# Two-layer post-LN transformer: the products of two attention steps follow each other, with a third probability buffer

## What is computed

```python
logits = jnp.einsum('btkgh,bskh->bkgts', q * scale, k)        # layer 0
probs = jax.nn.softmax(logits.astype(jnp.float32), axis=-1).astype(logits.dtype)
encoded = jnp.einsum('bkgts,bskh->btkgh', probs, v)
...
scores = jnp.einsum('bnqd,bnkd->bnqk', q, k) * scale          # layer 1
scores = jnp.where(causal, -jnp.inf, scores)
attn = jax.nn.softmax(scores, axis=-1)
out = jnp.einsum('bnqk,bnkd->bnqd', attn, v)
```

## Time and profile before

| | |
|---|---|
| runs | 854.34 us median of 3 (853.07 to 855.31) |
| profiled execution | span 851.4 us from the first to the last instruction; the page gives no other time of it |
| TensorE | 767.9 us busy (90%) |
| VectorE | 446.6 us busy (52%) |
| ScalarE | 359.7 us busy (42%) |
| POOL | 115.4 us busy (14%) |
| DMA | 75.01 MB, mean 88 GB/s |
| attention of layer 0 | first products at 44.9, last at 257.1 us |
| attention of layer 1 | first scores at 508.1, last products at 797.3 us |

### The profile page before, as it was taken

The page is one execution under the profiler, slowest core; times in us unless marked ns, Lnnn a source line. Parts: engine busy times, 40 slices in busy tenths (PEclk is TensorE's granted clock), DMA queues, the critical chain, the costliest instruction groups (busy, mean ns, idle before and its releaser), DMA issues. The chain is left out here.

```text
span 851.4 us, 11512 instructions
## 1 busy us (share of the span) xinstructions
PE 767.9 (90%) x3907; PEld 409.4 (48%) x3908; DVE 446.6 (52%) x1198; ACT 359.7 (42%) x565; POOL 115.4 (14%) x127
## 2 busy tenths in 40 slices
PE   5599999999999999999997879888998989989886
PEld 3222444444435556666665445434464445533675
DVE  2744554565435622222247676868765674662453
ACT  3389775685684012212223233444423442156030
POOL 0000000000000311111842411231011110022000
PEclk9699999999999999999999899989999999999999
DMA  7567207005107161111125870006300370000000
GB/s 217 148 204 223 93 26 209 27 25 149 38 26 247 43 198 46 43 45 46 32 84 169 251 201 2 1 27 187 110 1 3 106 216 1 2 1 26 14 12 26
DMA packets 51582, 75.01 MB, mean 88 GB/s; under 512 B 7607, under 2 KB 44763, under 8 KB 49227
## 3 DMA queue, kind: packets, MB, share of 16 engines
q1 hardware_dynamic: 49660, 69.26, 27.0%
q0 software_dynamic: 1872, 5.11, 2.2%
HBM read 46.57 MB, written 27.66 MB: 87 GB/s over the span
## 5 line engine op out<-in xcount | busy, mean ns | idle before, releaser
L656 PE MATMUL ps<-arena 128*128 128x256 f32 (+3 forms) x1084 | 326.7, 450 | 18.2 <-issue 2.9
L656 PEld LDWEIGHTS ps<-arena 128*128 128x128 f32 x1084 | 201.2, 195 | 106.6 <-issue 68.7
L970 ACT ACTIVATE arena<-ps 128x1024 f32<-128x1024 f32 x128 | 124.2, 1027 | 32.9 <-PE ps L711 32.6
L1067 ACT ACTIVATE arena<-ps 128x1024 f32<-128x1024 f32 (+3 forms) x128 | 82.9, 702 | 114.1 <-PE ps L903 114.0
L1450 DVE TENSOR_REDUCE arena<-ps 128x1 f32<-128x512 f32 (+3 forms) x176 | 100.4, 633 | 28.5 <-PE ps L881 27.6
L769 PE MATMUL ps<-arena 128*128 x184 | 86.5, 593 | 0.6 <-DVE arena L1177 0.6
L711 PE MATMUL ps<-arena 96*128 96x512 bf16 x256 | 71.4, 390 | 7.0 <-DMA arena<-q_stacks_dram 3.9
L1565 POOL TENSOR_SCALAR_AFFINE_SELECT arena<-arena 128x512 f32<-128x512 f32 x64 | 41.7, 652 | 253.3 <-ACT arena L1067 253.3
L725 PE MATMUL ps<-arena 128*32 128x512 f32 x512 | 69.6, 611 | 2.9 <-DVE arena L1223 2.7
L879 PE MATMUL ps<-arena 96*128 96x128 bf16 (+3 forms) x256 | 62.3, 303 | 9.6 <-DVE arena L1450 5.7
L648 PE MATMUL ps<-arena 128*128 128x128 f32 (+3 forms) x237 | 38.6, 302 | 23.3 <-DVE arena L1216 10.5
(11 more groups left out here) (153 smaller groups left out, 678.4 us busy)
## 6 DMA issues: line engine op xcount, KB each, us to landing
arena<-stacks_dram SPq DMA_DIRECT2D x16, 768.0 KB, 5.9
arena<-in_gate_up_proj SPq DMA_DIRECT2D x8, 1024.0 KB, 9.3
arena<-q_stacks_dram SPq DMA_DIRECT2D x8, 768.0 KB, 5.8
stacks_dram<-arena SPq DMA_DIRECT2D x16, 384.0 KB, 3.3
arena<-in_down_proj SPq DMA_DIRECT2D x8, 512.0 KB, 8.7
stacks_dram<-arena SPq DMA_DIRECT2D x16, 256.0 KB, 3.3
q_stacks_dram<-arena SPq DMA_DIRECT2D x8, 384.0 KB, 4.1
yg_dram<-arena SPq DMA_DIRECT2D x23, 128.0 KB, 1.7
```

The source lines that it names most:

```text
L656: last = nc.tensor.matmul(dst[0:rows, lo:hi], a, w, start=(n == 0), stop=(n == len(pairs) - 1))
L970: nc.scalar.activation(probs[:, 2 * p:2 * p + 2, :], ps[:, 2 * p:2 * p + 2, :], ACT.Exp)\
L1067: nc.scalar.activation(cprobs[:, i % 2, 2 * p:2 * p + 2, P * kt:S], ps[:, 2 * p:2 * p + 2, P * kt:S], ACT.Exp).then_inc(exp_done[p], 1)
```

## The change

`attention_order()` now goes through a batch in pairs of steps. For the pair i, i+1 (k its first step): scores of k+2, slot i, products of k and of k+1, scores of k+3, slot i+1. The slot tables are the same. In layer 0 (`crosses` true) this runs across the batch boundary; in layer 1 the last pair of a batch takes its products first, then the scores of k+2, slot 15, the scores of k+3. Layer 0 has a third probability buffer in expert 6's part of `gu`, so its load moves behind the attention, ahead of expert 7's. In layer 1 there is one buffer for each key tile, of its real width, where the last shares its place with the second; the exponentials' waits follow. The order of the steps on the other engines changes in the same way, since all walk the same steps.

```diff
+    scores(0)
+    scores(1)
     for b, fill in enumerate(fills):
...
+        for i in range(0, n, 2):
+            k = b * n + i
+            turn = i == n - 2 and not crosses
+            if not turn:
+                scores(k + 2)
+            steps += expand(fill[i], b, m)
+            steps += [(name + "P", b, i), (name + "P", b, i + 1)]
+            scores(k + 2 if turn else k + 3)
+            steps += expand(fill[i + 1], b, m)
+            if turn:
+                scores(k + 3)
...
-        probs1 = gu[:, E - 1, :, :].rearrange("p c (a n) -> p (c a) n", a=2)
+        probs1, probs2 = (gu[:, e, :, :].rearrange("p c (a n) -> p (c a) n", a=2) for e in (E - 1, E - 2))
...
+        def probs_of(k):
+            return (probs0, probs1, probs2)[k % 3]
+
+        def cprobs_of(kt):
+
+            at = cprobs_at + (0, 4 * S, 4 * (2 * S - P), 4 * S)[kt]
+            return arena[:, at:at + 4 * (S - P * kt)].rearrange("p (g n) -> p g n", g=4)
...
             layer0_stacks(2)
-            gate_up_load((6,))
             xs_store(1)
             layer0_stacks(3)
             xs_store(2)
 
             sp.wait_ge(pv_done, head0 * B)
-            gate_up_load((7,))
+            gate_up_load((6, 7))
...
-                    if head0 * b + i >= 2:
-
-                        act.wait_ge(pv_done, head0 * b + i - 1)
-                    probs = (probs0, probs1)[i % 2]
+                    if head0 * b + i >= 3:
+
+                        act.wait_ge(pv_done, head0 * b + i - 2)
+                    probs = probs_of(head0 * b + i)
...
-                    if headc * b + i >= 2:
+                    if kt % 2 and headc * b + i >= 2:
 
                         act.wait_ge(pv_done, head0 * B + headc * b + i - 1)
+                    elif kt % 2 == 0 and headc * b + i >= NT:
+                        act.wait_ge(pv_done, head0 * B + headc * b + i - 3)
```

More of the change, by code:

```diff
@@ L115, in expand, with attention_order, scores @@
     return steps
-def attention_order(fills, name):
+def attention_order(fills, name, crosses):
     steps = []
-    last = B * NT * HG - 1
+    n = NT * HG
+    def scores(k):
+        if k < B * n:
+            steps.append((name + "S", k // n, k % n))
+    scores(0)
+    scores(1)
     for b, fill in enumerate(fills):
@@ L124, in attention_order @@
         *fill, rest = fill.split("|")
-        assert len(fill) == NT * HG and not rest.strip()
-        for i, names in enumerate(fill):
-            k = b * NT * HG + i
-            if k == 0:
-                steps.append((name + "S", b, i))
-            if k < last:
-                steps.append((name + "S", (k + 1) // (NT * HG), (k + 1) % (NT * HG)))
-            steps += expand(names, b, m)
-            steps.append((name + "P", b, i))
+        assert len(fill) == n and not rest.strip()
+        for i in range(0, n, 2):
[9 more added lines that the diff above has]
+                scores(k + 3)
         assert m[0] in (0, len(MAXES)), m
@@ L138, in a_order @@
 def a_order():
-    return (expand(A_START, 0, [0]) + attention_order([A_FIRST, A_SECOND, A_THIRD, A_LAST], "att")
+    return (expand(A_START, 0, [0]) + attention_order([A_FIRST, A_SECOND, A_THIRD, A_LAST], "att", True)
             + expand(A_END, B, [0]))
 def c_order():
-    return (expand(C_START, 0, [0]) + attention_order([C_FIRST, C_SECOND, C_THIRD, C_LAST], "catt")
+    return (expand(C_START, 0, [0]) + attention_order([C_FIRST, C_SECOND, C_THIRD, C_LAST], "catt", False)
             + expand(C_END, B, [0]))
@@ L336, in post_ln_layers @@
         cparts = place([2, 3, S], BF16)
-        qf = [place([S])]
-        cprobs = place([2, 4, S])
+        cprobs_at = top[0]
+        place([4 * (S + S - P + S - 2 * P)])
         co_sb = place([HG, S])
@@ L341, in post_ln_layers @@
         top[0] = raw_end
-        qf += [place([S])]
+        qf = [place([S])]
         assert top[0] <= small_at, (top[0], small_at)
         top[0] = end_a
+        qf += [place([S])]
         qscr = nc.dram_tensor("q_stacks_dram", [B, 2, 6, P, S], BF16).ap()
@@ L725, in _ @@
                         last = nc.tensor.matmul(ps[32 * g:32 * g + 32, 4, :], v_aug[:, kt, hg, :],
-                                                (probs0, probs1)[i % 2][:, g, :], start=(kt == 0), stop=(kt == NT - 1))
+                                                probs_of(k)[:, g, :], start=(kt == 0), stop=(kt == NT - 1))
                     last.then_inc(pv_done, 1)
@@ L917, in _ @@
                                                 cv_aug[:, b % 2, kt, 4 * hg + g, :],
-                                                cprobs[:, i % 2, g, P * kt:S], start=(kt == 0), stop=(kt == NT - 1))
+                                                cprobs_of(kt)[:, g, :], start=(kt == 0), stop=(kt == NT - 1))
                     last.then_inc(pv_done, 1)
@@ L1563, in _ @@
                     pool.wait_ge(exp_done[1], k + 1)
-                    diag = cprobs[:, i % 2, :, P * kt:P * (kt + 1)]
+                    diag = cprobs_of(kt)[:, :, 0:P]
                     nc.gpsimd.affine_select(out=diag, in_=diag, compare_op=ALU.is_ge, fill=0.0, base=0,
```

2 lines of the change are left out of this document (1 added, 1 removed).

## The result

The changed kernel takes 892.64 us (median of 4 runs, 892.34 to 893.91) against 854.83 us (853.07 to 856.15) of the kernel before, measured beside it: a ratio of 1.044, interval 1.042 to 1.047. Slower, as forecast, but three times as much: 37.8 us where the prediction said 12.5, and outside its range.

A forecast was written before the change was run, and what follows sets the result against it. TensorE and ScalarE were taken as about equally loaded where slots are empty, TensorE alone bounding full ones. Terms -7.4 + 20.6 - 6.0 - 2.6 + 5.7 + 2.2 + 0 + 0 = +12.5 on 854.34 gave 867 us, range 853 to 874.

The forecast's parts named there:

- switches: Layer 0: each pair of products saves 0.24 us of matmul form changes; 31 pairs give -7.4.
- exponentials, added and removed: Layer 0: score steps wait for exponentials behind empty or short odd slots, +20.6; 20 present waits of about 0.30 go, -6.0.
- values at batch starts: Layer 0, batches 1 and 2: the first product's wait for values, 2.7 in all, is nearly all covered, -2.6.
- stacks: Layer 0: the next batch's first score step asks earlier and waits for its stacks, +5.7 (bounds 0 and 9).
- clock: Half clock for about 5 us behind the 4.7 us stack wait, +2.2, nothing elsewhere (bounds 0 and 5).
- The sum of 0: Layer 1: -5.0 + 1.4 + 2.8 + 0.8 = 0, as long as before; bounds -5 and +4.
- -5.0 for 21 pairs: Layer 1: 21 of 31 pairs save 0.24 us each; where VectorE bounds, a saved switch is worth nothing.
- the batch ends: Layer 1, three batch ends: score steps 16 to 18 follow with almost nothing between, +1.3, 0.8 and 0.7, 2.8 in all.
- Masks and the evacuations have the same count and size: Other engines: masks and evacuations unchanged, third buffer's effect hidden behind the scores, 0 in all.
- Rival 3: The clock falls in the 13 empty pairs of layer 0, up to +30, 880 to 897 us; chance 0.05.
- Loads: Expert 6's load, moved behind attention 0, takes 2.8 us, hidden ahead of the store: 0; without that cover +2.8.
- Rivals 1, 2 and 4: 1: exponentials' waits unpaid, about 839, 0.14; 2: stacks and clock hidden, 855 to 861, 0.18; 4: no net change, 0.06.

The follow-up runs named there:

- e3: The changed kernel with both attentions in the old order, third probability buffer and late expert 6 load kept; 853.15 us, 0.9985 of the kernel before.
- e1: The changed kernel with pairs in layer 0's attention alone, layer 1 in the old order; 872.90 us, 1.023 of the kernel before.
- e9: e8 with GpSimd's gathers of batch 3's expert rows issued behind the mask of step 18; 856.19 us, 1.002 of the kernel before.
- e8: The changed kernel with layer 0 in the old order and layer 1 paired except steps 12 to 15 of batches 0 to 2; 860.40 us, ratio 1.008.
- e2: The changed kernel with pairs in layer 1's attention alone, layer 0 in the old order; 874.65 us, 1.024 of the kernel before.
- e4: e1 with the first score step of each next batch behind the batch's last pair; 866.04 us, 1.015 of the kernel before.
- e5: The changed kernel with unread matmuls added in layer 0's stack waits at the ends of batches 1 and 2; 892.41 us, ratio 1.046.
- e6: The changed kernel with 8 unread matmuls ahead of the transposes of the maxima at layer 1's three later batch ends; 898.53 us, ratio 1.050.
- e10: The changed kernel with GpSimd's gathers of batch 3's expert rows issued behind the mask of step 18; 891.23 us, ratio 1.042.

## Why the prediction was wrong, step by step

**What bounds the kernel.** Right. The loop between TensorE and ScalarE and the two numbers 1.78 and 2.69 gave the empty pair at 5.1; it takes 5.09.

**Layer 0, term by term**, forecast against the groups above:

| term | forecast | in the traces |
|---|---|---|
| switches | -7.4 | -7.4 (31 x 0.24, as timed at full clock) |
| exponentials, added and removed | +20.6 - 6.0 = +14.6 | +14.9 (idle time, 1.7 to 16.6; from start to start 5.9 to 22, +16) |
| values at batch starts | -2.6 | -1.2 (2.7 to 1.5) |
| stacks | +5.7 | +9.5 (3.9 to 13.4) |
| clock | +2.2 | +8.3 (2.8 to 11.2, the estimate above) |
| sum | +12.5 | +24 to 25; the end of the attention moved by 24.2 |

The largest term was right to 0.3 us by idle time and to 1.5 from start to start. The switches were right: two products take 1.86 instead of 2.00, and a score step takes 0.87 where no product follows it, for 0.97; the products' busy time shows only 4.0 of it, since two pairs at half clock took 3.2 back. The values were mis-sized: the wait of batch 1 (1.23) is gone, that of batch 2 (1.44) stays, 1.48 after. The stacks were right for batch 2 (5.04 for 4.7) and too small for batch 1: 2.89, where I had counted 1.0. The rest, 1.6, is the very first score step, whose stacks landed later in this execution than in the one of before (5.51 for 3.90), which the order of steps doesn't touch. The clock fell in three places instead of one, and the start of the attention ran at half clock until 52.7 us instead of 46.5. That last part, 2.3 of the 8.3, isn't shown to come from the order: in e3, with the old order, it lasts until 49.7, in e1, with the paired one, until 48.8.

**Layer 1: the step that failed.** The sum of 0 rested on three things.

The first: -5.0 for 21 pairs, those outside the stretches where VectorE bounds. The products' busy time fell by 4.0, but e9, with the batch ends single and the gathers moved, gains 0.7 us in batch 1 and 0.8 in batch 3 against e3, and loses at the start and in batches 0 and 2. So the 5.0 never showed.

The second: the batch ends were priced at 2.8 us from the score steps alone. e8 against e2 measures 14.3, clock included. I had looked at what the score steps wait for, and not at what the products that moved ahead had been covering: the 2.15 us from the last maximum to its transposes, which were in the trace of before.

The third: "Masks and the evacuations have the same count and size". They do, but a count says nothing of a queue. Step 17's mask stands behind four gathers on GpSimd, and the pair takes away the 8 us that hid it: 4.2 us where the batch ends are single (e9), a wait of 1.2 us in the change itself. The queue stood still, and the one who waits for it came earlier. The same holds of the evacuations: the products' waits for them grew by 3.1 us.

**The clock, in both layers.** "+2.2 behind the 4.7 us wait and nothing elsewhere" is the term that failed most. By the estimate above it is 8.3 us in layer 0 and 12.8 in layer 1, 21.1 together. That is 18.9 more than I gave it, most of the 29.8 us by which the two attentions passed their forecast in the traces. The forecast had a rival for it and put it in the wrong place. Rival 3 wanted the clock to fall in the empty pairs, and the profile of the change says no: from 52.7 to 151.7 us, five empty pairs of batch 0 among it, and from 267.8 on, with the last ones of batch 3, it stays at 1.00, with 0.74 and 0.31 us of idle time in each pair. It fell behind single longer waits, 5.04, 2.89 (ahead of the first score step of batch 2, at 150.24) and 1.93 us. One fall is between the two, from 264.4 to 267.8 in batch 3, behind a pair whose slots held only four transposes and the router's products of 8 columns:

```profile
260.71 0.60 PE L729 MATMUL ps<-arena 96*128 96x512 bf16 x2 [0.30 <-ACT arena L988]
261.62 0.60 PE L729 MATMUL ps<-arena 96*128 96x512 bf16 x2 [0.31 <-ACT arena L988]
262.15 1.92 PE L674 MATMUL ps<-arena 128*128 128x8 f32 x16
264.01 3.36 PE L743 MATMUL ps<-arena 128*32 128x512 f32 x16
```

The pair of products takes 3.3 us there instead of 1.86. e4's fall at 89.4 us is of the same kind, behind short waits alone. The length of one wait does not settle it either: in the change itself the products wait 2.11 us for VectorE twice, at 614.92 with a fall behind it (from 615.9) and at 712.96 with none. The rule of the Trainium skill, TensorE: Matmul & The Clock Gate, HAM oscillation, that idle stretches between bursts bring the lower clock back, agrees with the longer waits of the change, and with most of the empty pairs it doesn't. I had given the rival built on it 0.05.

**Loads.** Right: e3 is not slower than before, and the late load of expert 6 is hidden.

**The step that failed, in short.** "Nothing elsewhere" for the clock (2.2 forecast, 21.1 by the traces) and the sum of 0 for layer 1 (18.1 in the traces, 21.5 by e2). The waits for stacks were too small by 3.8 besides.

**Rivals.** Rivals 1, 2 and 4 are refuted: the waits for exponentials are paid in full, and stacks and clock are not hidden. Of rival 3 the time range is right (880 to 897) and the mechanism is not.

## What to carry to other kernels

Before moving work forward, list for each moved instruction what it stood beside, on every engine: a product may be free where it is because it covers another engine's last 2 us, and its partner may depend on a queue that nobody had to wait for until now. Price a new TensorE wait twice, once for the wait and once for the work behind it at 1.2 GHz; at the end of batch 1 of layer 1 the wait was 1.93 us (0.82 before) and the down product behind it took 1.7 more. Keep busy time and clock apart: a group's busy time falls by what an order saves and rises by what the clock takes. On a loop between two engines pairing can pay only if what stands between the pairs is longer than the round trip (here 1.37 us of work), and even then the 12 pairs of layer 0 saved 2.9 us at the products and gave back 3.0 in waits for exponentials.

## What the runs showed of the hardware

That removing a fall of the clock at one place need not shorten the kernel: e5 kept the clock at 1.00 from 50.7 to 258.9 us and won 3.3 us there in its trace, while its median stayed; e6 kept two down products at 3.6 us from start to start instead of 5.3 and 6.4, and had as much half clock in layer 1 as the change (44.4 us), at other places. Which stretch falls to half clock depends on more than the wait in front of it: the same program place, the pair at 264 us, fell in all six kernels with layer 0 paired, those with other waits before it too (e1 at 260.4, e4 at 253.2, e5 at 258.9, e6 at 263.3, e10 at 260.8, each 17 to 18 us ahead of its attention's end).

And that a change of matmul form has a price: at full clock the four column-group products of 512 columns take 1.00 us when scores follow, two such steps in a row 1.86, and a score step takes 0.97 ahead of them for 0.87 ahead of transposes.
